# One program region for attention and mixture, the last quad's deviation inside the mixture, and the first turn of the routing weights directly ahead of the expansion

## The reference

```python
h = _L0_tok_ref(x, ...)                                   # token features, MLP with gelu
h = h + _L0_attn_ref(_layernorm(h, axis=-1), ...)         # neighbourhood attention, 31 keys, dilation 2
h = h + _L0_ffn_ref(_layernorm(h, axis=-1), ...)          # mixture of 8 experts, top 2
h = h + _L1_attn_ref(_layernorm(h, axis=-1), ...)         # attention with decay
h = h + _L1_ffn_ref(_layernorm(h, axis=-1), ...)          # soft mixture of experts

def _moe(tokens, router_w, w1, b1, w2, b2):
    logits = tokens @ router_w.T
    rw, re = jax.lax.top_k(jax.nn.softmax(logits, axis=-1), 2)
    rw = rw / jnp.maximum(rw.sum(-1, keepdims=True), 1e-12)
    combine = jnp.zeros((N, E)).at[jnp.arange(N)[:, None], re].set(rw)
    out = tokens
    for e in range(E):
        h = jax.nn.gelu(tokens @ w1[e] + b1[e], approximate=False)
        out = out + combine[:, e:e + 1] * (h @ w2[e] + b2[e])
    return out
```

## Time and profile before

| | |
|---|---|
| median of 3 runs | 876.51 us (876.44 to 878.71) |
| profiled execution | 880.86 us |
| its span | 879.10 us |
| PE busy | 804.4 us (92%) |
| DVE, ACT, POOL busy | 583.7, 476.7, 301.2 us |
| mixture, from its first matmul to the next stage | 380.4 to about 566 us |

### The profile page before, as it was taken

The page is one execution under the profiler, slowest core; times in us unless marked ns, Lnnn a source line. Parts: engine busy times, 40 slices in busy tenths (PEclk is TensorE's granted clock), DMA queues, the critical chain, the costliest instruction groups (busy, mean ns, idle before and its releaser), DMA issues. The chain is left out here.

```text
span 879.1 us, 28915 instructions
## 1 busy us (share of the span) xinstructions
PE 804.4 (92%) x12642; PEld 410.5 (47%) x12648; DVE 583.7 (66%) x854; ACT 476.7 (54%) x656; POOL 301.2 (34%) x292
## 2 busy tenths in 40 slices
PE   3989799999999999679999799799998899999996
PEld 2232377776776776413333233376663333333332
DVE  5547477777776776637777955477673377777776
ACT  2254377778778777346565656412221455555553
POOL 3235453633534423202443454473453710000000
PEclk9999799999999999979999999999999999999998
DMA  4210221002001001020000220053321011111111
GB/s 108 27 30 1 85 73 31 4 5 63 4 4 64 4 4 65 1 61 1 1 2 1 83 63 1 18 164 98 95 83 41 13 33 44 47 49 49 49 50 37
DMA packets 38670, 36.38 MB, mean 41 GB/s; under 512 B 20817, under 2 KB 25074, under 8 KB 38418
## 3 DMA queue, kind: packets, MB, share of 16 engines
q1 hardware_dynamic: 37474, 32.52, 13.1%
q10 hardware_dynamic: 1072, 2.02, 0.7%
HBM read 18.79 MB, written 7.34 MB: 30 GB/s over the span
## 5 line engine op out<-in xcount | busy, mean ns | idle before, releaser
L2233 ACT ACTIVATE se_a<-se_p,cols 128x512 f32<-128x512 f32 x128 | 92.8, 775 | 75.9 <-PE se_p L2186 75.9
L2253 DVE SCALAR_TENSOR_TENSOR se_a<-se_p,cols,z 128x1024 f32<-128x1024 f32 x64 | 82.2, 1284 | 48.8 <-PE se_p L2196 48.8
L1273 DVE TENSOR_REDUCE na_rowmax<-na_ps 128x16 f32<-128x1024 f32 x64 | 78.1, 1220 | 54.0 <-PE na_ps L1111 54.0
L1604 ACT ACTIVATE z<-me_p,cols 128x512 f32<-128x512 f32 x128 | 81.1, 685 | 59.4 <-PE me_p L1533 54.6
L1735 DVE TENSOR_TENSOR me_gw<-me_pc,z 128x1024 f32<-128x1024 f32 x64 | 78.3, 1223 | 46.7 <-PE me_pc L1547 38.3
L947 POOL TENSOR_TENSOR z<-na_k,const 128x512 f32<-128x512 f32 x62 | 62.5, 1040 | 129.6 <-ACT na_k L1192 129.6
L488 POOL TENSOR_TENSOR n_sq<-h 128x512 f32<-128x512 f32 x64 | 68.4, 1074 | 94.6 <-DVE h L858 40.0
L1563 PE MATMUL me_py<-me_gw,w_out 64*64 64x512 f32 x512 | 88.8, 601 | 0.0
L1533 PE MATMUL me_p<-z,moe_w 64*64 64x512 f32 x512 | 82.8, 621 | 6.4 <-issue 3.8
L535 POOL TENSOR_TENSOR z<-h,n_bc 128x512 f32<-128x512 f32 x58 | 75.1, 1306 | 25.7 <-DMA n_bc<-n_spread 25.6
L1276 DVE TENSOR_TENSOR z<-na_ps,na_rowmax 128x1024 f32<-128x1024 f32 x64 | 78.4, 1225 | 2.2
(11 more groups left out here) (359 smaller groups left out, 1290.2 us busy)
## 6 DMA issues: line engine op xcount, KB each, us to landing
n_bc<-n_spread SPq DMA_DIRECT2D x116, 128.0 KB, 3.1
z<-z SPq DMA_DIRECT2D x64, 128.0 KB, 2.4
out<-se_rows SPq DMA_DIRECT2D x16, 256.0 KB, 2.1
n_spread<-n_rstd SPq DMA_DIRECT2D x12, 256.0 KB, 2.0
const<-in_const ACTq DMA_DIRECT2D x1, 1114.0 KB, 8.2
const<-in_const ACTq DMA_DIRECT2D x1, 562.0 KB, 4.2
f_w<-in_L_ffn_W SPq DMA_DIRECT2D x4, 128.0 KB
const<-in_const ACTq DMA_DIRECT2D x1, 258.0 KB, 3.0
```

Of the source, the lines that this page charges most:

```text
L1273: nc.vector.tensor_reduce(rowmax[b][:], scored, AX, ALU.max).then_inc(s_max, 1)
L1604: nc.scalar.activation(g[at.n % 7][:, b, :], hidden(at.n, b)[:], ACT.Gelu, bias=col(s, "moe_b1", ep)).then_inc(s_g, 1)
L2233: nc.scalar.activation(a1[at.k % 2][:, e2, :], hidden(at.n, e2)[:], ACT.Relu, scale=col(s, "f1_g1", 2 * ep + e2), bias=col(s, "f1_be1", 2 ...
L2253: nc.vector.scalar_tensor_tensor(out=a2[at.k % 2][:], in0=p_2[:], scalar=col(s, "f1_be2", ep), in1=s.f1_w[:, ep, :].unsqueeze(1).broadcast ...
```

## The change

- `neighbourhood_attention` and `mixture_of_experts` write into one block. The barrier between them is gone; semaphores of both live until the end of the block.
- Routing buffers and the chain of the first ranking move into `route_buffers` and `chained`. `first_ranked` keeps four steps ahead of the last residual; the other steps are `rank_on`, ahead of all of DVE's rounds. The first ranking takes the weights by Tanh, as the later quads do, in place of Exp, reciprocal and product. Its Tanh stands on ACT behind GELU 2. The first turned logits use another PSUM bank (`p_s[1][:, 1]`), and the ranking's scratch lies in other rows of `s.z`, so GELU 6 waits for the ranking.
- PE: the warming matmuls and the last variance behind attention's loops go. In the mixture `first` of rounds 0 to 5 has two warming matmuls (before: three in rounds 0 and 1), and behind round 4 stands the variance of quad `LAST`, which ACT copies out of PSUM behind GELU 4.
- ACT: Ln and Exp of quad `LAST` run in loop 8 of the mixture (`last_deviations`).
- The first turn and its two fetches move from lead 4 to lead 3, directly ahead of the first expansion.
- POOL: rows 12 to 15 are rescaled two at a time at its rows 2 and 3.
- The logits of the second quad wait for attention's last residual, and the first `second` for the copied variance.

```diff
-            keep_warm(nc, s, p_o[:], 5)
-            variance_of(LAST)
-            keep_warm(nc, s, p_o[:], 4)
...
-            sc.wait_ge(s_gap, 1)
-            nc.scalar.activation(gap, gap, ACT.Exp, scale=-1.0).then_inc(s_less, 1)
-            deviations_of(LAST)
...
-            unrolled(TURNS, 2, (4, maximum(0)), (4, maximum(1)), (3, normalise), (1, residual), (1, route))
-            next_ranked()
+            unrolled(TURNS, 2, (4, maximum(0)), (4, maximum(1)), (3, normalise), (1, residual), (1, route))
...
-        block = ctx.enter_context(nc.Block())
+        s_last = outer.enter_context(nc.semaphore("me_last"))
...
-                if p < 4:
-                    rescale(1, 4 * LAST + p)
+                if 2 <= p < 4:
+                    rescale(1, 4 * LAST + 2 * (p - 2))
+                    rescale(1, 4 * LAST + 2 * (p - 2) + 1)
...
-                if p >= 8:
-                    pool.wait_ge(s.n_var, quad(2, p // 4 - 2))
+                pool.wait_ge(s.n_var, quad(2, p // 4 - 2) if p >= 8 else quad(1, LAST - 1 + p // 4))
...
                     if c == 1:
-                        te.wait_ge(s_route, linked_to(0, 1))
+                        te.wait_ge(r.s_h, done(NP - 1))
...
-                if at.n < 2:
-                    keep_warm(nc, s, p_c[:, 0, :], 3)
+                if at.n < 6:
+                    keep_warm(nc, s, p_c[:, 1, :], 2)
+                if at.n == 4:
+                    te.wait_ge(s.n_sq, nth(1, NP - 1))
+                    variance(nc, s, LAST, p_y[:, 1, :]).then_inc(s.n_var, 1)
...
+                if at.n == 0:
+                    te.wait_ge(s_last, 1)
...
-            unrolled(EP * NP, 16, (4, turn), (AHEAD_G, while_ahead(first)), (BEHIND_G, when_behind(first)), (3, expand), (2, second), (AHEAD, logits_of), (0, spreads))
+            unrolled(EP * NP, 16, (4, turn), (AHEAD_G, while_ahead(first)), (BEHIND_G, when_behind(first)), (3, first_turn), (3, expand), (2, second), (AHEAD, logits_of), (0, spreads))
...
+                if at.n == 6:
+                    sc.wait_ge(s_ctin, done(0))
                 for b in range(2):
                     nc.scalar.activation(g[at.n % 7][:, b, :], hidden(at.n, b)[:], ACT.Gelu, bias=col(s, "moe_b1", ep)).then_inc(s_g, 1)
+                if at.n == 2:
+                    sc.wait_ge(s_gap, done(0))
+                    nc.scalar.activation(r.gap, r.gap, ACT.Tanh, scale=0.5).then_inc(s_tanh, 1)
+                if at.n == 4:
+                    sc.wait_ge(s.n_var, quad(1, LAST))
+                    nc.scalar.activation(s.rstd[:, LAST, :], p_y[:, 1, :], ACT.Copy).then_inc(s_last, 1)
+
+            def last_deviations(at):
+                if at.n == 8:
+                    sc.wait_ge(s_last, 1)
+                    nc.scalar.activation(s.rstd[:, LAST, :], s.rstd[:, LAST, :], ACT.Ln, bias=s.eps[:]).then_inc(s.n_ln, 1)
+                    sc.wait_ge(s.n_ln, 2 + LAST)
+                    nc.scalar.activation(s.rstd[:, LAST, :], s.rstd[:, LAST, :], ACT.Exp, scale=-0.5).then_inc(s.n_rstd, 1)
...
+            rank_on()
             unrolled(EP * NP, 16, (3, weigh), (2, residual), (AHEAD, router))
```

More of the change, by code:

```diff
@@ L911, in sem @@
         def sem(name):
[L912 removed]
+            return outer.enter_context(nc.semaphore("na_" + name))
         TURNS = 2 * NP
@@ L928, in neighbourhood_attention @@
         s_first, s_near = sem("s_first"), sem("near")
[L929 to L933, removed]
+        p_route = p_s[1][:, 1].rearrange("p h a w -> p (h a w)")
+        s_rl, s_lt, s_rt = [sem(x) for x in ("rl", "lt", "rt")]
         p_first = p_t[:, 0:4, :].rearrange("p g c -> p (g c)")
-        block = ctx.enter_context(nc.Block())
+        r.s_h = s_h
         @block.gpsimd
         def _(pool):
-            nc.gpsimd.memset(r.ct_in[:], 0.0).then_inc(s_zero, 1)
+            nc.gpsimd.memset(r.ct_in[:], 0.0).then_inc(r.s_zero, 1)
             give_credits(pool, s_blk)
@@ L1317, in first_ranked @@
[L1317 to L1341, removed]
@@ L1343, in route @@
+                linked(v.tensor_reduce(r.first_of, r.logits, AX, ALU.max))
+                linked(v.tensor_tensor(r.best, r.logits, over_experts(r.first_of), ALU.is_equal))
+                linked(v.tensor_tensor(r.best, r.best, rank_of(s), ALU.mult))
             def route(at):
@@ L1360, with route_buffers, chained, linked @@
 LINKS = 21
-def route_buffers(nc, ctx):
+def route_buffers(nc, s, ctx):
     r = Buffers()
     r.ct_in = ctx.enter_context(nc.sbuf_tensor("me_ctin", [128, 4, 2, 2, 2, ROUTES], F32))
+    r.logits_t = row(s.z, NB - 2)
+    r.logits, r.best, r.masked, r.picked, r.weights = [row(s.z, n)[:, c:c + 256].rearrange("p (g e) -> p g e", e=NE)
+                                                       for n, c in ((NB - 1, 0), (NB - 1, 256), (NB - 4, 0), (NB - 4, 256), (NB - 3, 0))]
+    r.first_of, r.second_of, r.top, r.gap, r.w_best, r.w_next = [row(s.z, NB - 3)[:, 256 + ROUTED * k:256 + ROUTED * k + ROUTED] for k in range(6)]
+    r.s_zero, r.s_link = [ctx.enter_context(nc.semaphore("r_" + x)) for x in ("zero", "link")]
+    r.links = 0
     r.high, r.middle = [ctx.enter_context(nc.sbuf_tensor("me_" + x, [128, ROUTED, NE], BF16)) for x in ("high", "middle")]
     return r
+def chained(ve, r):
+    def linked(ins):
+        ins.then_inc(r.s_link, 1)
+        r.links += 1
+        ve.wait_ge(r.s_link, r.links)
+    return linked
 def over_experts(x):
@@ L1583, in _ @@
             give_credits(sc, s_ct, s_parts, s_g, s_copied, s_odd)
-            for x in (s_lt, s_tanh):
-                sc.sem_inc(x, done(0))
+            give_credits(sc, s_tanh)
+            sc.sem_inc(s_lt, done(0))
             def router(at):
```

116 lines of the change are left out of this document (73 added, 43 removed).

## The result

The changed kernel takes 871.09 us (median of 10 runs, 869.13 to 875.46), the one before 877.23 us (10 runs): a ratio of 0.994, 95% interval 0.992 to 0.996. Forecast were 870.0 us and a ratio of 0.993. The profiled execution has a span of 873.7 us (before: 879.1) and took 875.3 us with what lies around it.

The account below looks back on a forecast made before the run. PE bounds the mixture, with time only at the seam. Start -11.4, prologue 0, stall +4.0, clock +1.7, cast -1.1, POOL +0.3 sum to -6.5 us: 870.0 us from a timed median of 876.51, range 865 to 875.

Parts of the forecast that it names:

- Start: Seam from attention to mixture: without the barrier PE starts round 0 at 369.0 instead of 380.40, -11.4 us.
- Prologue: Round 0 to first expansion: 15.9 us as now, the saved slow clock paying for moved-in work; 0 us.
- The inserts: Work moved into PE's prologue lengthens rounds: routing logits +0.65, transposes +0.2, last variance +0.6 us; together between 0 and 3.1.
- 2.3 us of slack: Prologue: weights ready by 380.1 and next logits copied by 380.6, ahead of round 6's GELU at 382.95.
- The first turn's new place: Turn behind round 6 costs nothing; its old place ahead of round 5 would make PE wait about 0.7 us.
- Stall in loop 8: Ln, Exp and three table loads hold ACT 5.2 us, so PE waits ahead of round 19: +4.0 us.
- Clock: Behind the loop 8 stall PE runs 3.4 us at half speed: +1.7 us, bounds 0 and 3.4.
- 3.4 us of slow running: Basis of the clock term: after 2.95 us idle, PE ran at clock 0.50 from 505.5 to about 508.9.
- Cast: DVE's cast to the weights' parts no longer runs beside a POOL rescale, shortening PE's expansion wait: -1.1 us, bounds 0 and 1.9.
- POOL busier later: DVE's steps with two SBUF operands in loops 12 to 16 may wait for POOL: +0.3 us, bounds 0 and 1.
- POOL's chain: Hop, spreads and rescales finish row 3's square about 1.3 us before PE's variance in loop 17; no wait, but thin.

Follow-up runs that it names:

- e12: Changed kernel with PE's round 0 held until DVE has made the gap of the first ranking: 880.20 us, ratio 1.002 to the kernel before.
- e5: Kernel before, with only GpSimd's rescales moved: none at its row 2, rows 14 and 15 both at its row 3. 878.52 us, ratio 1.001.
- e8: Changed kernel with PE's first turn and both of ACT's fetches back at lead 4, ahead of round 5: 871.96 us, ratio 0.994 to the kernel before.
- e1: Changed kernel with Ln and Exp in loop 8 replaced by two copies of the same size: 865.46 us, ratio 0.987 to the kernel before.
- e2: Changed kernel with the table holding both Ln and Exp loaded by name ahead of Ln in loop 8: 869.03 us, ratio 0.990 to the kernel before.
- e3: Changed kernel with 14 warming matmuls ahead of round 19, in PE's idle stretch: 871.09 us, ratio 0.993 to the kernel before.
- e9: The changed kernel itself, unaltered, measured a second time: 874.55 us, ratio 0.997 to the kernel before.
- e7: Changed kernel with PE's lead cut from 9 to 6 in loop 8, to 4 in loop 33, and Ln and Exp's common table named at both blocks: 871.28 us.
- e11: Changed kernel with PE's lead stepped 9, 6, 4, Ln and Exp's common table named at both blocks, and loop 8's block moved to loop 9: 873.80 us.

## Why the prediction was right, step by step

- **Start, -11.4 us:** measured -11.60. e12 gives 4.6 us of it back, and they count in full. One reading in it was wrong: PE waits for ACT's credits, but these do not wait for the end of the table load. PE started at 369.50 while the load ran until 369.68; in e5, where nothing else holds it, 0.19 us ahead of the load's end. In the changed kernel the credits, by e5's 1.09 us due at 369.49, and the end of the projection come at the same moment, so the rows do not tell which of them PE followed. Why the credits come 1.1 to 1.3 us behind the start of the load is open.
- **Prologue, 0:** 15.74 against 15.90, -0.16; but +0.63 against the 15.11 of e5, the old prologue in another execution. That the clock saved pays for what moved in holds within that spread. The inserts measured 0.66 (logits), 0.11 (transposes) and 0.67 us (variance), against 0.65, 0.2 and 0.6. The weights had 2.3 us of slack, as worked out: the turn could start at 380.98 and started at 383.30.
- **The first turn's new place, 0:** this step failed. I priced the wait at the turn in the old place and overlooked that in the new one the transposes and ACT's fetch stand between round 6 and the expansion. PE waits 1.28 us there; the old place is 0.74 us faster to the first expansion (e8). The error did not show in the sum, since I had counted that path, GELU 6 and the fetch included, and never set it against the old place.
- **Stall in loop 8, +4.0 us:** 4.08 by the markers; 4.01, 4.02 in two profiles. e1 shows that the block on ACT is its cause, e2 that one load is worth 1.28 us of it.
- **Clock, +1.7 us:** 2.45 us in the first profile, 1.72 in the second. The mechanism is shown by e3 beside the five profiles with an unfilled stall; the size moves from one execution to the next (1.4 to 2.5 us in the five). 3.4 us of slow running was one sample, and e3 shows the same wait with none. In that sample the granted clock is 0.99 in 505 to 506 and 0.50 in 506 to 507: it fell half a us behind the wait, not with it. With 0.80 in 509 to 510 it came back at 509.4, so the length of 3.4 us was read rightly. Behind the stall it was about 5 us in the first profile.
- **Cast, -1.1 us:** -1.14, and -1.07 by itself in e5. The Trainium skill ("GPSIMD Engine Reference", section "1. Specifications") says that GpSimd shares its SBUF interfaces with VectorE, and contends with VectorE's instructions that have two SBUF inputs or run in a two-port mode; the trace agrees in that the cast takes 0.28 us alone and 1.35 beside a rescale. The cast has one SBUF input, so by that page it would have to be in a two-port mode; no row here names the mode.
- **POOL busier later, +0.3 us:** +0.38; +0.66 in e9, of which 0.25 and 0.56 us are waits of PE for DVE. DVE's steps with two SBUF inputs take up to 0.81 and 1.09 us beside POOL there, 0.42 in the kernel before.
- **POOL's chain, slack 1.3 us:** its slack was larger. From Exp's end to the first rescale it took 5.8 us (418.54 to 424.33), not 7.4, and row 3's square ended 3.6 us ahead of the variance of loop 17. That this chain is next in line is shown by e1, e7 and e11.

```profile
424.33 1.27 POOL L535 TENSOR_TENSOR z<-h,n_bc 128x512 f32<-128x512 f32 x1 [14.57 <-DMA n_bc<-n_spread]
...
437.19 1.04 POOL L488 TENSOR_TENSOR n_sq<-h 128x512 f32<-128x512 f32 x1
```

The sum was -6.5, and the markers give -6.0 (183.22 against 189.21). The timed medians give -6.1 in the first comparison and -3.2 in the second, with the same two kernels, though e9's profile has the stretch no longer than the first (182.72). A part of the spread is the clock; a difference between chips is possible and was not tried. So there is luck in how near 871.09 lies to 870.0: the second median, 874.55, is inside the range of 865 to 875 only just. What is shown more firmly is the sum by the markers, and there the errors partly cancel: the clock cost up to 0.75 us more than forecast, the start gained 0.2 and the prologue 0.16.

## What to carry to other kernels

The barrier between these two stages cost the whole tail that stood in front of it, and each of its pieces had to go somewhere: 11.6 us were won, and 6.5 us of them (5.8 in e9) went back because a 1.3 us computation on ACT was put, with three table loads, into a place where PE had 0.4 us of room. Where Ln and Exp stand between other functions, name the table that has both. Before a stall is hidden, ask what is next: here it was GpSimd's wait for a DMA, and e11, which hid the stall, met a wait of 4.75 us there.

## What the runs showed of the hardware

- Two calls of the same two functions made two table loads or one, depending on whether the common set was named (e2: 1.28 us less on ACT, and 1.28 us less of PE's stall). The Ln started 0.02 us behind its load's end (414.18 behind 412.88 + 1.28). The Trainium skill ("ScalarE: Activation LUTs", section "What ACT_TABLE_LOAD costs") counts a drain beside each load; no row here shows one.
- Behind 4.0 us of idleness PE's matmuls ran at 1.2 GHz at once in one execution and one round later in another (1.98 and 1.09 us for round 19); behind 2.73 us (e2) they stayed at 2.4 GHz. Behind the same 2.95 us at loop 33 they fell to 1.2 GHz in the kernel before and stayed at 2.4 GHz in e3.
- In e5 PE started on ACT's credits 0.19 us ahead of the end of the table load that stands before them on ACT (378.17 against 377.08 + 1.28 = 378.36).
